# One change to the attention of a Mamba and attention block: GpSimd's first guess in two parts, two score buffers for three heads, and a shorter split of the attention inputs

## The reference, cut to what matters

```python
x = x + 0.5 * _L0_ffn_ref(_layernorm(x), ...)
x = x + _L0_attn_ref(_layernorm(x), ...)          # Mamba2 scan, 128 heads
x = x + 0.5 * _L0_ffn_ref(_layernorm(x), ...)
x = x + 0.5 * _L1_ffn_ref(_layernorm(x), ...)
x = x + _L1_attn_ref(_layernorm(x), ...)          # here
x = x + 0.5 * _L1_ffn_ref(_layernorm(x), ...)

# _L1_attn_ref: H = 32 heads of HD = 16, HKV = 8 key and value heads
qr, kr = apply_rope(q, cos, sin), apply_rope(k, cos, sin)
draft = einsum('bhqd,bhkd->bhqk', qr, kr) + causal
_, draft_indices = jax.lax.top_k(draft, 128)      # of each row of 1024
mask = 0 at draft_indices, else -inf; also -inf where causal_future
scores = einsum('bhqd,bhkd->bhqk', qr, kr) / 4 + mask
attn = softmax(scores)
out = einsum('bhqk,bhkd->bhqd', attn, v)
return out.reshape(B, Sq, 512) @ Wo.T
```

## Time and profile before

| | |
|---|---|
| median of 3 runs | 3170.42 us (3167.81 to 3173.41) |
| the profiled execution | 3171.23 us, span 3169.4 us |
| busy share PE, DVE, ACT, POOL | 88%, 78%, 62%, 52% |
| ScalarE's sweeps, L2093, 896 instructions | 734.8 us busy |
| the power function in `move`, L2186, 128 instructions | 193.3 us busy, 1510 ns each |

### The profile page before, as it was taken

One profiled execution on the slowest core, in us unless ns is written; L12 is line 12 of the kernel. 1 busy time (PEld: TensorE's weight loads), 2 busy tenths in 40 slices (PEclk: granted clock), 3 DMA queues, 4 the chain that ended last, 5 costly groups with the idle time before them and its releaser, 6 DMA issues. The chain is left out here.

```text
span 3169.4 us, 50416 instructions
## 1 busy us (share of the span) xinstructions
PE 2798.6 (88%) x15722; PEld 1527.9 (48%) x15833; DVE 2467.5 (78%) x4664; ACT 1952.2 (62%) x4186; POOL 1649.7 (52%) x3659
## 2 busy tenths in 40 slices
PE   8899999999999999999999989837777777777769
PEld 4455455455454464554554544514444444444444
DVE  5678687697696795786876977848999899998846
ACT  2464554564564554545545533569999999999823
POOL 3236245264263263362452544767777777777503
PEclk9999999999999999999999999958989899989889
DMA  2222122232232132231221320000000000000010
GB/s 90 66 80 94 70 97 80 73 107 70 77 116 84 63 104 80 77 103 67 90 90 60 100 75 1 28 1 2 2 2 2 2 2 2 2 2 2 1 51 27
DMA packets 65804, 169.62 MB, mean 54 GB/s; under 512 B 11776, under 2 KB 19328, under 8 KB 64512
## 3 DMA queue, kind: packets, MB, share of 16 engines
q1 hardware_dynamic: 54448, 115.17, 11.2%
q10 hardware_dynamic: 11088, 51.19, 4.6%
HBM read 161.08 MB, written 5.24 MB: 52 GB/s over the span
## 5 line engine op out<-in xcount | busy, mean ns | idle before, releaser
L2093 ACT ACTIVATE X<-ah_z,ah_trial 128x256 bf16<-128x256 f32 (+6 forms) x896 | 734.8, 829 | 51.4 <-POOL ah_trial L2194 41.9
L1207 ACT ACTIVATE m_mix<-m_mix,m_cs 128x128 f32<-128x128 f32 x1024 | 312.9, 388 | 253.6 <-DMA m_mix<-cs_rows 253.6
L1089 POOL TENSOR_TENSOR m_xdec<-m_xdt,m_decay_out 128x512 f32<-128x512 f32 x112 | 143.7, 1283 | 213.1 <-DVE m_xdt L1333 202.1
L2263 DVE TENSOR_SCALAR_CACHE_REDUCE X<-ah_z,ah_cut 128x256 bf16<-128x256 f32 (+6 forms) x224 | 193.7, 875 | 74.0 <-POOL ah_cut L2199 74.0
L1117 POOL TENSOR_TENSOR m_squares<-m_squares 128x256 f32<-128x256 f32 x128 | 108.3, 846 | 274.4 <-ACT m_squares L1219 274.4
L1013 PE MATMUL m_ps_d<-m_w_out,m_gate 128*128 128x512 f32 x512 | 235.2, 602 | 0.0
L1013 PE MATMUL m_ps_x<-m_w_out,m_gate 128*128 128x512 f32 x512 | 233.6, 599 | 0.0
L2104 ACT ACTIVATE X<-ah_ps_e 128x512 f32<-128x512 f32 (+3 forms) x384 | 185.7, 485 | 38.0 <-PE ah_ps_e L2015 27.8
L1975 PE MATMUL ah_ps_m<-a_kT,a_qT 128*128 128x512 bf16 (+3 forms) x318 | 106.2, 365 | 115.2 <-DVE tables L2292 114.7
L2284 DVE MAX8 ah_top<-ah_ps_m 128x8 f32<-128x256 f32 (+6 forms) x224 | 185.5, 828 | 22.6 <-PE ah_ps_m L1979 21.2
L2254 DVE TENSOR_SCALAR_CACHE_REDUCE ah_z<-ah_ps_z 128x256 f32<-128x256 f32 (+6 forms) x224 | 182.7, 816 | 15.9 <-PE ah_ps_z L1958 15.8
(11 more groups left out here) (326 smaller groups left out, 7483.2 us busy)
## 6 DMA issues: line engine op xcount, KB each, us to landing
m_mix<-cs_rows SPq DMA_DIRECT2D x128, 512.0 KB, 4.4
m_w_proj<-in_w_proj ACTq DMA_DIRECT2D x69, 512.0 KB, 3.3
m_fade<-fade_rows SPq DMA_DIRECT2D x224, 128.0 KB, 2.9
m_w_out<-in_w_out ACTq DMA_DIRECT2D x7, 2048.0 KB, 7.8
X<-in_x SPq DMA_DIRECT2D x8, 256.0 KB, 5.1
m_w_out<-in_w_out SPq DMA_DIRECT2D x1, 2048.0 KB, 10.0
x_away<-X SPq DMA_DIRECT2D x1, 2048.0 KB, 7.3
X<-x_away SPq DMA_DIRECT2D x8, 256.0 KB, 6.1
```

Of the source, the lines that this page charges most:

```text
L1207: act.activation(mix[:, u % 3, h, :], mix[:, u % 3, h, :], ACT.Relu, bias=cs[:, c, h0 + h:h0 + h + 1], scale=-1.0).then_inc(lag_done, 1)
L2093: act.activation(sign[:, at % 2, 0:(t + 1) * P], z[:, h % RING, cols(t)], ACT.Sign, bias=trial[:, h % RING, 0, t - 1:t], scale=-1.0, accum ...
L2263: dve.tensor_scalar(mark[:, (h * W + t) % 2, 0:(t + 1) * P], z[:, h % RING, cols(t)], cut[:, h % 2, t - 1:t], 0.0, ALU.is_ge, ALU.add, acc ...
```

## The change

Three edits, and two small ones inside `move`.

1. `first_cut` is cut into `first_spread` (mean, variance, root, and the far bracket; six instructions) and the rest. `first_spread(n+1)` now stands behind the first move of the round, the rest behind the second. `split_max` still comes first. In `move` one comparison writes two tiles at once in place of two, one wait between two products goes, and the last product but one no longer needs the power function's result, so that it is issued while that runs or right behind it.
2. For heads 29, 30 and 31, whose iterations no longer use `ps_z` for new scores, the marked scores of t = 5 and 7 go to `ps_z`, those of 4 and 6 to `ps_m`. From t = 5 on, `marked_scores` of t waits for the pick of t-2.
3. In the attention inputs the second subtraction writes the third part directly in bf16, on VectorE and GpSimd. The third cast goes, and `rest` shrinks to one plane. The copy to `q_tok` moves from VectorE to ScalarE, behind its five copies of the turned tile; VectorE waits for it (`q_kept`) before it writes part 0 of the next tile.

The diff, cut to its core:

```diff
         qk_sin = sb("qk_sin", [P, HEADS, AD])
-        rest = sb("rest", [P, 2, W])
+        rest = sb("rest", [P, W])
         part = sb("part", [P, 3, W], BF16)
...
                         act.activation(out, ps_t[n][:], ACT.Copy).then_inc(out_done, 1)
+                if t < NT:
+                    act.wait_ge(q_split, 4 * t + 1)
+                    act.activation(q_tok[:, t], by_head[:, 0, 0:AH, :], ACT.Copy).then_inc(q_kept, 1)
...
             cols = slice(heads.start * AD, heads.stop * AD)
-            src = (qk_cos[:].rearrange("p h d -> p (h d)"), rest[:, 0], rest[:, 1])[n]
+            src = (qk_cos[:].rearrange("p h d -> p (h d)"), rest[:])[n]
             if n:
-                engine.wait_ge(split_done, 5 * t + 2 * n)
+                engine.wait_ge(split_done, 4 * t + 2)
             engine.tensor_copy(part[:, n, cols], src[:, cols]).then_inc(split_done, 1)
-            engine.wait_ge(split_done, 5 * t + 2 * n + 1)
-            if n < 2:
-                engine.tensor_tensor(rest[:, n, cols], src[:, cols], part[:, n, cols], ALU.subtract).then_inc(split_done, 1)
+            engine.wait_ge(split_done, 4 * t + 2 * n + 1)
+            left = part[:, 2, cols] if n else rest[:, cols]
+            engine.tensor_tensor(left, src[:, cols], part[:, n, cols], ALU.subtract).then_inc(split_done, 1)
...
                 split(pool, k_split, K_HEADS, t, 1)
-                split(pool, k_split, K_HEADS, t, 2)
+                pool.wait_ge(k_split, 4 * t + 4)
                 if t >= 1:
...
                 for n, lo, hi in Q_RUNS:
-                    split(dve, q_split, Q_HEADS, t, n)
-                    if n == 0:
-                        dve.tensor_copy(q_tok[:, t], by_head[:, 0, 0:AH, :]).then_inc(q_kept, 1)
-                        if t >= 1:
-                            dve.wait_ge(turned, GROUPS * t)
+                    if n == 0 and t:
+                        dve.wait_ge(q_kept, t)
+                    if n < 2:
+                        split(dve, q_split, Q_HEADS, t, n)
+                    else:
+                        dve.wait_ge(q_split, 4 * t + 4)
+                    if n == 0 and t:
+                        dve.wait_ge(turned, GROUPS * t)
                     dve.tensor_copy(stacked[:, 0:AH, lo:hi, :],
...
         m_at = lambda t: BANK * ((t + 1) % 2) if t < 4 else 0
+        two_buffers = lambda h, t: h >= AH - 3 and t >= 4
+        in_z = lambda h, t: two_buffers(h, t) and t % 2 == 1
+        marked_in = lambda h, t: ps_z if in_z(h, t) else ps_m
...
                 L, at = (t + 1) * P, m_at(t)
+                out = marked_in(h, t)
                 pe.wait_ge(take_done, h * W + t)
-                done = h * W + t - 1 - (1 < t < 4)
+                done = h * W + t - 1 - (1 < t < 4 or two_buffers(h, t) and t > 4)
+                if in_z(h, t):
+                    pe.wait_ge(z_done, AH * NT)
                 if done:
...
                     if diagonal:
-                        pe.matmul(ps_m[:, at + L - P:at + L], env.ident_bf[:], env.future_bf[:], start=True, stop=False,
+                        pe.matmul(out[:, at + L - P:at + L], env.ident_bf[:], env.future_bf[:], start=True, stop=False,
                                   skip_group_check=True)
-                    pe.matmul(ps_m[:, at + n:at + n + w], qT[:, h, t * P:(t + 1) * P], kT[:, h // REP, n:n + w],
+                    pe.matmul(out[:, at + n:at + n + w], qT[:, h, t * P:(t + 1) * P], kT[:, h // REP, n:n + w],
                               start=not diagonal, stop=False, skip_group_check=True)
...
                     w = min(BANK, L - n)
-                    last = pe.matmul(ps_m[:, at + n:at + n + w], ident_taken[:], mark[:, (h * W + t) % 2, n:n + w], start=False, stop=True,
+                    last = pe.matmul(out[:, at + n:at + n + w], ident_taken[:], mark[:, (h * W + t) % 2, n:n + w], start=False, stop=True,
                                      skip_group_check=True)
...
-            def first_cut(h):
+            def first_spread(h):
...
                 pool.wait_ge(own, at + 6)
+                steps[0] = at + 6
+
+            def first_cut(h):
+
+                at, r = steps[0], h % RING
                 pool.tensor_tensor(offset, root, table[:, 0], ALU.mult).then_inc(own, 1)
                 pool.tensor_tensor(reach, root, table[:, 1], ALU.mult).then_inc(own, 1)
-                pool.wait_ge(own, at + 7)
+                pool.wait_ge(own, at + 1)
                 pool.tensor_tensor(trial[:, r, 0], mean, offset, ALU.add).then_inc(guessed, 1)
-                pool.wait_ge(own, at + 8)
+                pool.wait_ge(own, at + 2)
                 pool.wait_ge(guessed, h + 1)
...
                 pool.tensor_tensor(bracket[:, r, 1, 0], trial[:, r, 0], reach, ALU.add).then_inc(own, 1)
-                pool.wait_ge(own, at + 10)
-                steps[0] = at + 10
+                pool.wait_ge(own, at + 4)
+                steps[0] = at + 4
...
                 pool.wait_ge(own, at + 1)
-                pool.tensor_scalar(side[:, 0], trial[:, r, 1], 0.0, None, ALU.is_lt).then_inc(own, 1)
+                pool.tensor_scalar(side[:, 0:3:2], trial[:, r, 1:2].to_broadcast([P, 2, W]), 0.0, None, ALU.is_lt).then_inc(own, 1)
                 pool.tensor_scalar(side[:, 1], trial[:, r, 1], 0.0, None, ALU.is_ge).then_inc(own, 1)
-                pool.tensor_scalar(side[:, 2], trial[:, r, 1], 0.0, None, ALU.is_lt).then_inc(own, 1)
                 pool.wait_ge(own, at + 4)
...
                                    side[:, 0:2].unsqueeze(2).to_broadcast([P, 2, 2, W]), ALU.mult).then_inc(own, 1)
-                pool.wait_ge(own, at + 5)
                 pool.tensor_tensor(kept[:], bracket[:, r], side[:, 1:3].unsqueeze(2).to_broadcast([P, 2, 2, W]),
...
                 pool.tensor_scalar(missed[:, 0], trial[:, r, 1], 2.0 * (TOPK - LEAST), None, ALU.is_gt).then_inc(own, 1)
+                pool.wait_ge(own, at + 6)
+                pool.tensor_tensor(bracket[:, r], kept[:], moved_in[:], ALU.add).then_inc(own, 1)
                 pool.wait_ge(own, at + 7)
-                pool.tensor_tensor(bracket[:, r], kept[:], moved_in[:], ALU.add).then_inc(own, 1)
+                pool.tensor_tensor(missed[:, 1], missed[:, 0], side[:, 0], ALU.add).then_inc(own, 1)
                 pool.wait_ge(own, at + 8)
-                pool.tensor_tensor(missed[:, 1], missed[:, 0], side[:, 0], ALU.add).then_inc(own, 1)
+                pool.tensor_tensor(between[:], bracket[:, r, 1], bracket[:, r, 0], ALU.subtract).then_inc(own, 1)
                 pool.wait_ge(own, at + 9)
-                pool.tensor_tensor(between[:], bracket[:, r, 1], bracket[:, r, 0], ALU.subtract).then_inc(own, 1)
+                pool.tensor_tensor(toward[:, 1], toward[:, 0], missed[:, 1], ALU.mult).then_inc(own, 1)
                 pool.wait_ge(own, at + 10)
-                pool.tensor_tensor(toward[:, 1], toward[:, 0], missed[:, 1], ALU.mult).then_inc(own, 1)
+                pool.tensor_tensor(slope[:, 0], between[:, 1], table[:, 5], ALU.pow).then_inc(own, 1)
                 pool.wait_ge(own, at + 11)
-                pool.tensor_tensor(slope[:, 0], between[:, 1], table[:, 5], ALU.pow).then_inc(own, 1)
+                pool.tensor_tensor(slope[:, 2], between[:, 0], toward[:, 1], ALU.mult).then_inc(own, 1)
                 pool.wait_ge(own, at + 13)
-                pool.tensor_tensor(slope[:, 1], between[:, 0], slope[:, 0], ALU.mult).then_inc(own, 1)
+                pool.tensor_tensor(slope[:, 1], slope[:, 2], slope[:, 0], ALU.mult).then_inc(own, 1)
                 pool.wait_ge(own, at + 14)
-                pool.tensor_tensor(slope[:, 2], slope[:, 1], toward[:, 1], ALU.mult).then_inc(own, 1)
-                pool.wait_ge(own, at + 15)
-                steps[0] = at + 15
+                steps[0] = at + 14
                 if k < COUNTS - 1:
-                    pool.tensor_tensor(trial[:, r, 0], trial[:, r, 0], slope[:, 2], ALU.add).then_inc(moved, 1)
+                    pool.tensor_tensor(trial[:, r, 0], trial[:, r, 0], slope[:, 1], ALU.add).then_inc(moved, 1)
                     pool.wait_ge(moved, MOVE_AT[h, k] + 1)
...
                         pool.wait_ge(take_done, (h - 1) * W)
-                    pool.tensor_tensor(cut[:, h % 2], trial[:, r, 0], slope[:, 2], ALU.add).then_inc(cut_done, 1)
+                    pool.tensor_tensor(cut[:, h % 2], trial[:, r, 0], slope[:, 1], ALU.add).then_inc(cut_done, 1)
                     pool.sem_inc(moved, 1)
...
                     split_max(n - 2)
-                if live(n + 1):
-                    first_cut(n + 1)
-                for back, k in SWEEPS:
+                for slot, (back, k) in enumerate(SWEEPS):
                     if live(n - back):
                         move(n - back, k)
+                    if live(n + 1) and slot == 0:
+                        first_spread(n + 1)
+                    if live(n + 1) and slot == 1:
+                        first_cut(n + 1)
...
                 dve.wait_ge(marked, at + 1)
```

(4 more changed lines are left out.)

2 lines of the change are left out of this document (1 added, 1 removed).

## The result

The changed kernel takes 3146.61 us, median of 4 runs (3143.98 to 3150.56), against 3170.43 for the kernel before in the same comparison (3167.81 to 3173.41, 4 runs). The ratio is 0.9926, 95% interval 0.9908 to 0.9943: 23.8 us less. The forecast of 3140.5 was 6.1 us too low; its range of 3126 to 3152 held the time.

The account below looks back on a forecast made before the run. The prediction took a ring through GpSimd's moves and guess to bound the heads loop, with a second ring close behind. Gains of 17.5 + 6.7 + 1.6 + 0.6 + 3.8 = 30.2 us gave 3140.5 us, range 3126 to 3152.

Parts of the forecast that it names:

- full rounds: Heads loop, 27 iterations between the takes of heads 2 and 29: 28.65 us each falls to 28.0, 17.5 us gained.
- first rounds: Start of the heads stage: ScalarE's waits of 9.56 and 2.36 us shrink to 4.7 and 0.6, 6.7 us gained.
- attention inputs: Stage of attention inputs: less VectorE and GpSimd work per tile shortens TensorE's waits, 3.8 us gained (2 to 5).
- The first ring: Heads loop: last sweep, move, split, guess, move, two sweeps; ScalarE's 1.15 us wait per round for a moved trial goes.
- The second ring: Heads loop: VectorE's take, its z writes, TensorE's chunk 1, ScalarE; margin 0.16 us, then a wait of 0.51 us a round.
- c: Heads loop: time from the end of a round's last sweep to VectorE's first take, 5.18 us, forecast to become 4.89.
- D: Heads loop: time from VectorE's first take to exponent chunk 1 ready, 27.45 us in one round, 28.10 in another.
- The move: GpSimd's move in the heads loop: one comparison and a wait less, 4.88 - 0.29 = 4.6 us.
- TensorE is the bound, at 7.90 us a tile: Attention inputs: without its waits for VectorE's k_sums copy TensorE sets the pace, 8.25 - 0.35 = 7.90 us a tile.
- (a): Rival, heads loop: chunk 1 isn't late and ScalarE alone sets 27.48 us a round, 31.6 us gained, 3126; chance 0.20.
- (b): Rival, heads loop: waiting for chunk 1 takes nearly everything, rounds of 28.4 us, 6.8 us gained, 3151; chance 0.18.
- (c): Rival, heads loop: the spread makes the third trial late for ScalarE's fourth sweep, margin 1.8 us; slower, 3200; chance 0.04.

Follow-up runs that it names:

- the order alone: Kernel before with only the guess split in two parts, its spread behind the first move and the rest behind the second: 3147.14 us, ratio 0.9927.
- chunk 1 ahead: Changed kernel with exponent chunk 1 computed on TensorE ahead of the next head's first scores instead of behind them: 3123.18 us, ratio to the kernel before 0.9845.
- the cast alone: Kernel before with only the subtraction writing the third part itself, no third cast; the q_tok copy stays on VectorE: 3173.62 us, one run.
- the copy alone: Kernel before with only the copy of q_tok moved from VectorE to ScalarE; the third cast stays: 3171.97 us, one run.

## Why the prediction was right, and where it was short

| term | forecast | profiled |
|---|---|---|
| full rounds | 17.5 | 773.57 - 758.55 = 15.0 |
| first rounds, first sweep to take of head 2 | 6.7 | 109.10 - 103.28 = 5.8 |
| two buffers | 1.6 | 33.49 - 31.43 = 2.1 |
| two last moves | 0.6 | 53.14 - 52.52 = 0.6 |
| attention inputs | 3.8 | 88.60 - 86.06 = 2.5 |
| sum | 30.2 | 26.0 |

The span fell by 24.1. The other 1.9 us lie where nothing is changed: the stage began 0.9 us later, and from the last exponent to the end it took 127.6 us in place of 126.6. Both scatter by more than that.

**The first ring** went as written: the wait of 1.15 us is gone with the order alone, and twice the shorter move would have taken only part of it.

**The second ring** gave the size. Its formula can be put as: a round is (own + c + D - 4.16) / 2, with ScalarE's own work 27.48. It holds where the rounds alternate, from the take of head 2 to that of head 26. There the twelve rounds with the long wait for chunk 1 have a D of 28.04 us on average, from the take to chunk 1 ready, and the takes ahead of them a c of 5.03, from the last sweep's end to the take. ScalarE's own work is 27.40 (chunk 1 ahead). That makes 28.16 us a round, and 28.15 is measured. In the rows above, D is 2484.72 - 2456.88 = 27.84 in one round and 2540.90 - 2512.96 = 27.94 in another.

So the step that was mis-sized is D first, and c, which is the move, second. D was 27.78 in the forecast, the middle of two rounds of the kernel before, and came out 0.26 longer; c was 4.89 and came out 0.14 longer. Halved, they are 0.13 and 0.07 us a round; the own work gives back 0.04. Over the 24 rounds that is 3.6 us lost, and the last three, which hardly wait, give 1.1 back: the 2.5 us that are missing. That c weighs little by itself the runs show too: with the order alone it is 5.20 on average and the takes stand 756.89 us apart, 1.7 less than with the shorter move. With one more power function in the spread it is 756.52 us. From round to round D moves between 26.7 and 28.3 us in the changed kernel up to head 28. Why it moves so is open, and that two rounds of the kernel before gave a D so near to it is in part luck.

**The move** lost 0.17 us, not 0.29. Groups by line of GpSimd after the change, from 2090 to 3060 us (busy us, mean ns | idle us just before them):

```profile
L2184 POOL TENSOR_SCALAR ah_side<-ah_trial 128x14 f32<-128x14 f32 x127 | 33.3, 262 | 0.0
...
L2187 POOL TENSOR_TENSOR ah_moved_in<-ah_trial,ah_side 128x28 f32<-128x28 f32 x127 | 30.8, 242 | 10.6
```

The comparison of two tiles costs 0.26 us; it was bounded well. The loss is behind it: `moved_in` had no idle time before (0.0), because the comparison it needs stood two instructions ahead. With one comparison gone it stands right ahead, and the product waits 10.6 / 127 = 0.08 us for its result. I costed the instruction that goes and not the cover that it gave to the one behind.

**First rounds.** The waits at the first sweeps were 9.56 and 2.36 us, and then 3.07, which the prediction left out; they are 4.98, 0.89 and 0.70, where 4.7 and 0.6 were forecast. The first take came 6.2 us sooner, and 0.4 us went again before the take of head 2. The two buffers came out within their scatter (1.0 to 2.2 us). The 0.6 us of the two last moves are not shown: between the takes of heads 29 and 31 four kernels with the old move take 52.6 to 52.7 us, three 53.1 to 53.2, and the changed one 52.52, so the number was met by luck.

**Attention inputs.** The failed step is "TensorE is the bound, at 7.90 us a tile". Timelines of VectorE, GpSimd and TensorE in one tile of the changed kernel:

```profile
2031.09 0.79 DVE L1640 COPY ai_stacked<-ai_part 128x1536 bf16<-128x1536 bf16 x1
...
2031.40 0.62 POOL L1611 COPY ai_k_one<-ai_part 128x128 bf16<-128x128 bf16 x1
...
2032.53 0.78 POOL L1597 TENSOR_TENSOR ai_part<-ai_rest,ai_part 128x128 bf16<-128x128 f32 x1
...
2033.38 1.70 POOL L1617 COPY ai_stacked<-ai_part 128x384 bf16<-128x384 bf16 x3
...
2034.72 0.35 PE L1538 MATMUL ai_ps_sum<-ai_k_one 128*16 128x17 bf16 x8 [0.17 <-DVE a_k_sums L1644]
...
2035.18 2.39 PE L1548 MATMUL ai_ps_t<-ident_bf,ai_stacked 128*128 128x128 bf16 x40
```

The same two copies, and GpSimd's second subtraction, in the kernel before:

```profile
2031.38 0.64 DVE L1634 COPY ai_stacked<-ai_part 128x1536 bf16<-128x1536 bf16 x1
...
2031.25 0.35 POOL L1608 COPY ai_k_one<-ai_part 128x128 bf16<-128x128 bf16 x1
...
2032.25 0.48 POOL L1594 TENSOR_TENSOR ai_rest<-ai_rest,ai_part 128x128 f32<-128x128 f32 x1
```

GpSimd's copy and second subtraction with the cast alone:

```profile
2031.06 0.35 POOL L1608 COPY ai_k_one<-ai_part 128x128 bf16<-128x128 bf16 x1
...
2032.05 0.48 POOL L1594 TENSOR_TENSOR ai_part<-ai_rest,ai_part 128x128 bf16<-128x128 f32 x1
```

TensorE's transposes stand 7.84 and 8.25 us apart by turns, 8.0 on average, against 8.4 before. In the short tiles TensorE waits for nobody, as forecast. In the long ones it still waits 0.17 us for VectorE's key sums, and then 0.11 us until GpSimd's stacking, which ends at 2035.08, lets the transposes start at 2035.18. So six tiles gave 2.2 us where 3.1 were forecast, and the last tile 0.3 where 0.7 were.

Part of what was meant to go came back by alignment. GpSimd's copy of `k_one` went from 0.35 to 0.62 us and its second subtraction from 0.48 to 0.78, beside a VectorE copy that itself went from 0.64 to 0.79. It is the copy of `q_tok` that does this: both GpSimd instructions are as long with the copy alone, and neither has grown with the cast alone. That is why the copy gives little beside the cast. It gains 0.9 us between tiles 1 and 6, and loses 0.4 us again in the first tile and 0.3 at the end. The Trainium skill, SBUF — State Buffer, "Who interferes with whom", says that VectorE's copies in their fast mode lock the port pair that GpSimd reads and writes through, and that whoever comes second stands still. By that rule the new alignment costs both engines at the two copies, and the trace agrees. The prediction had named the other rule of that section, for subtractions, with 0.31 us; the second subtraction grew by 0.30. It then said that TensorE's 7.90 us would cover it; in every second tile, and in the first, they did not.

**The rivals.** (a), ScalarE alone, did not come by the change; it is what chunk 1 ahead brings (27.40 for a forecast of 27.48). (b) did not come either, since the takes are 758.55 apart, under 766. (c) was 1.5 us away, close to what was forecast: one power function uses it up, two turn the gain into a loss. GpSimd's instructions hardly grew: the two products of the move behind the power function, of which the earlier trace rows shows the first at 207 ns, have means of 214 and 203.

## What to carry to other kernels

Two waits lay in rings over the same engine here, and an edit to the second was worth nothing until the first was gone, and all of it after that (0 and 23 us for the same two lines). So write down each ring with the margin of the next, and try the reorder again once the ring ahead is cut. When an instruction is dropped from a chain of dependent short ones, ask whose result it covered.
